# Gated cross-attention with FFN: the way from attention to FFN in halves, and the first query maxima with bv·Wo ahead of the first barrier

## What is computed

```python
# attention, added to x through a gate
q = rope(layernorm(x) @ Wq.T + bq); k = rope(ctx @ Wk.T + bk); v = ctx @ Wv.T + bv
x1 = x + tanh(g_xattn) * ((softmax(q k^T / 4) v) @ Wo.T + bo)
# FFN with fake quantisation, added through a second gate
h  = layernorm(x1)
xq = quant(h, sigmoid(clip_x) * max(abs(h)) / 127)          # ONE maximum over all 8 batches
p  = silu(xq @ quant_rows(w_gate).T) * (xq @ quant_rows(w_up).T)
hq = quant(p, sigmoid(clip_down) * max(abs(p)) / 127)        # again one maximum over everything
out = x1 + tanh(g_ffn) * (hq @ quant_rows(w_down).T)
```

## Time and profile before

| what | value |
|---|---|
| runs shown | 617.42, 615.32, 617.26 us, median 617.26 |
| the profiled execution | 615.77 us, span of its core 614.0 us |
| block A, B, C in the span | 0 to 107.3, 107.6 to 516.1, 516.4 to 614.0 us |
| busy share | PE 90%, DVE 87%, ACT 73%, POOL 43% |
| granted TensorE clock, mean | 0.96 of full |

### The profile page before, as it was taken

One profiled execution on the slowest core, in us unless ns is written; L12 is line 12 of the kernel. 1 busy time (PEld: TensorE's weight loads), 2 busy tenths in 40 slices (PEclk: granted clock), 3 DMA queues, 4 the chain that ended last, 5 costly groups with the idle time before them and its releaser, 6 DMA issues. The chain is left out here.

```text
span 614.0 us, 18320 instructions
## 1 busy us (share of the span) xinstructions
PE 554.1 (90%) x6473; PEld 259.5 (42%) x6478; DVE 531.4 (87%) x679; ACT 445.5 (73%) x886; POOL 263.9 (43%) x372
## 2 busy tenths in 40 slices
PE   6999997899899989999999999999999973988485
PEld 3555654244344424444444444444445321333264
DVE  3899989899999969899899899899899746689888
ACT  2667766247777867897897897897897771788694
POOL 7699996701233434214214314324323210899300
PEclk9999999569999989999999999999999997899889
DMA  8759877523432333242342243253240000000035
GB/s 291 238 164 294 242 203 203 154 55 68 81 65 64 77 61 63 55 89 63 57 89 62 59 86 63 60 85 61 62 90 8 2 2 1 0 2 0 0 104 172
DMA packets 61255, 55.20 MB, mean 90 GB/s; under 512 B 11040, under 2 KB 58784, under 8 KB 61216
## 3 DMA queue, kind: packets, MB, share of 16 engines
q1 hardware_dynamic: 61216, 54.70, 36.1%
HBM read 37.62 MB, written 16.78 MB: 89 GB/s over the span
## 5 line engine op out<-in xcount | busy, mean ns | idle before, releaser
L857 ACT ACTIVATE prob<-st_ps 128x512 f32<-128x512 f32 x512 | 281.2, 596 | 71.9 <-PE st_ps L716 64.9
L916 DVE TENSOR_REDUCE negm<-mx_ps 128x2 f32<-128x1024 f32 x256 | 300.1, 1206 | 17.6 <-PE mx_ps L724 17.4
L716 PE MATMUL st_ps<-q,k 98*32 98x512 bf16 x2048 | 182.5, 385 | 4.4 <-ACT prob L857 4.0
L724 PE MATMUL mx_ps<-k,q 96*32 96x512 bf16 x2048 | 164.8, 396 | 7.5 <-DVE negm L916 3.8
L748 PE MATMUL pv_ps<-prob,v_u 128*32 128x512 f32 x1024 | 133.7, 594 | 1.4 <-ACT prob L857 1.4
L716 PEld LDWEIGHTS st_ps<-q,k 98*32 98x32 bf16 x2048 | 58.6, 96 | 94.6 <-ACT prob L857 40.5
L724 PEld LDWEIGHTS mx_ps<-k,q 96*32 96x32 bf16 x2048 | 55.3, 98 | 79.3 <-DVE negm L916 25.5
L1084 POOL TENSOR_TENSOR msplit<-negm,onesf 128x16 bf16<-128x16 f32 x32 | 7.1, 221 | 135.6 <-DVE negm L916 125.7
L1104 POOL TENSOR_TENSOR normal<-turned,recip 128x256 f32<-128x256 f32 x32 | 19.9, 621 | 79.9 <-DVE recip L930 79.9
L748 PEld LDWEIGHTS pv_ps<-prob,v_u 128*32 128x32 f32 x1024 | 32.1, 111 | 27.3 <-ACT prob L857 3.0
L298 POOL TENSOR_TENSOR parts<-work 128x512 bf16<-128x512 f32 x32 | 38.4, 1206 | 7.1 <-DVE work L286 6.1
(11 more groups left out here) (126 smaller groups left out, 709.5 us busy)
## 6 DMA issues: line engine op xcount, KB each, us to landing
qk_parts<-parts SPq DMA_DIRECT2D x96, 128.0 KB, 2.8
k<-qk_parts SPq DMA_DIRECT2D x192, 64.0 KB, 2.8
q<-qk_parts SPq DMA_DIRECT2D x192, 64.0 KB, 2.9
ctx<-in_ctxT SPq DMA_DIRECT2D x8, 512.0 KB, 4.5
X<-in_x SPq DMA_DIRECT2D x8, 512.0 KB, 7.7
out<-X SPq DMA_DIRECT2D x7, 512.0 KB, 2.9
q<-mrow SPq DMA_DIRECT2D x64, 4.0 KB, 2.5
wf<-in_w_down SPq DMA_DIRECT2D x1, 704.0 KB, 5.0
```

Of the source, the lines that this page charges most:

```text
L716: last = nc.tensor.matmul(score_bank(i)[lo:lo + COLS, :], k6[g][:, h, kt * P + lo:kt * P + lo + COLS], q6[g][:, h, :], start=True, stop=True)
L724: last = nc.tensor.matmul(pair[lo:lo + COLS, qt % 2, :], q6[g][0:ROWS, h, qt * P + lo:qt * P + lo + COLS], k6[g][0:ROWS, h, :], start=True ...
L857: nc.scalar.activation(prob[kt % 2][:, h, :], score_bank(HPU * kt + h)[:], ACT.Exp, scale=SCALE).then_inc(exp_done, 1)
L916: nc.vector.tensor_reduce(negm[g % 2][:, lo:lo + 2], pair[:], op=ALU.max, axis=AX.X, negate=True).then_inc(mx_read, 1)
```

## The change

In block A, after the last projection, GpSimd makes `bv_rep`, TensorE does bv·Wo into a bank of `k_ps` and then the first two pairs of query scores into the banks of `xT_ps` and `v_ps` (which `mx_ps` now is), and ScalarE copies bv·Wo out. In block B VectorE no longer has the two steps of `bo_b`: GpSimd does them, after it has split the maxima of unit 0.

For batch 7, the products with `attnT[0]` are issued in the last unit (`project_last(hf, 0)`), and only those with `attnT[1]` after the last `weigh`. The statistics and normalisation of batch 6 move into the last batch, all on VectorE but `rstd`; ScalarE's eight passes over batch 6, six in the last batch and two behind it, go. Batch 7 is normalised in halves: ScalarE the first two tiles, VectorE the last two, with `rstd` in two halves of two columns on GpSimd.

In block C, chunk 0 is scaled half by VectorE and half by ScalarE, clipped in two halves, transposed into two banks and copied out by ScalarE and VectorE together; chunk 1 is scaled by GpSimd instead of ScalarE.

```diff
@@ block A, TensorE after the last pair of batches
+                pe.wait_ge(bv_ready, KC)
+                pe.wait_ge(rot_ready, 4 * (B - 1) + 2)
+                for c in range(KC):
+                    last = nc.tensor.matmul(k_ps[:, 0, 0:D], bv_rep[:, c, :], wo_raw[:, c, :], start=(c == 0), stop=(c == KC - 1))
+                last.then_inc(wobv_ready, 1)
+                pe.wait_ge(unit_in[0], NLOAD)
+                pe.wait_ge(xnT_ready, KC * B)
+                query_scores(0, 0, 0, mx_ps[0])
+                pe.wait_ge(v_kept, 2 * B)
+                query_scores(0, 0, 1, mx_ps[1])
@@ block A, ScalarE
+                act.wait_ge(wobv_ready, 1)
+                nc.scalar.activation(bo_b[:], k_ps[:, 0, 0:D], ACT.Copy).then_inc(wobv_kept, 1)
@@ block B, TensorE: the last projection in two parts
+                def project_last(hf, c):
+                    dst = project_bank(B, hf)
+                    pe.wait_ge(attnT_ready, 2 * (B - 1) + c + 1)
+                    if c == 0:
+                        pe.wait_ge(x1_ready, 2 * (B - 1))
+                    for t in range(2):
+                        for lo in range(0, P, COLS):
+                            last = nc.tensor.matmul(dst[lo:lo + COLS, t * D:(t + 1) * D], attnT[c][:, (2 * hf + t) * P + lo:(2 * hf + t) * P + lo + COLS], woT[:, c, :],
+                                                    start=(c == 0 and t == 0), stop=(c == KC - 1), skip_group_check=True)
+                    if c == KC - 1:
+                        last.then_inc(wo_ready, 1)
...
+                            if is_last(b) and g == 3 and kt >= 2:
+                                project_last(kt - 2, 0)
...
-                            wait_if(pe, mx_read, 8 * g + 2 * h + j - 1)
-                            query_scores(0, g, h, j, mx_ps[j])
-                        if g == 0 and h >= 2:
...
+                            if g or h:
+                                pe.wait_ge(mx_read, 8 * g + 2 * h + j - 1)
+                                query_scores(g, h, j, mx_ps[j])
...
                 for hf in range(2):
-                    project(B, hf)
+                    project_last(hf, 1)
@@ block B, VectorE
-                dve.wait_ge(wobv_ready, 1)
-                nc.vector.tensor_tensor(bo_b[:], wobv_ps, bo_raw[:], ALU.add).then_inc(bo_ready, 1)
...
-                x1_normalise(B - 2, lambda t: mean[:, TPB * (B - 2) + t:TPB * (B - 2) + t + 1])
-                x1_largest(B - 2)
-                for hf in range(2):
-                    residual(B, hf)
-                    x1_statistics(hf)
...
+                residual(B, 0)
+                x1_statistics(B - 1, (0, 1))
+                residual(B, 1)
+                x1_moments(B - 1, 0)
+                x1_statistics(B - 1, (2,))
+                x1_statistics(B - 1, (3,))
+                dve.wait_ge(tail_scaled, 3)
+                nc.vector.scalar_tensor_tensor(shift1[:], moments1[:, 1, 0:2, 0], -1.0, rstd[:, NT - TPB:NT - TPB + 2], ALU.mult, ALU.mult).then_inc(tail_shift, 1)
+                x1_moments(B - 1, 1)
+                x1_normalise(B - 1, 1)
+                dve.wait_ge(tail_half, 2)
+                x1_half_largest(0)
+                dve.wait_ge(xn_done, TPB * (B - 1) + 2)
+                x1_half_largest(1)
@@ block C, ScalarE, VectorE and GpSimd at its start
-                nc.scalar.activation(xi[1], V[:, 4:8, :], ACT.Copy, scale=ainv[:, 0:1]).then_inc(xs0_ready[1], 1)
-                keep_chunk(0)
+                nc.scalar.activation(xi[0][:, 2:4, :], V[:, 2:4, :], ACT.Copy, scale=ainv[:, 0:1]).then_inc(xs0_ready[1], 1)
+                act.wait_ge(xqT0_ready, 1)
+                nc.scalar.activation(xqT[0][:, 0, :], xqT0_ps[0], ACT.Copy).then_inc(xqT0_kept, 1)
...
-                nc.vector.tensor_scalar(xi[0], V[:, 0:4, :], ainv[:, 0:1], None, ALU.mult).then_inc(xs0_ready[0], 1)
-                clip_x(0, 0)
+                nc.vector.tensor_scalar(xi[0][:, 0:2, :], V[:, 0:2, :], ainv[:, 0:1], None, ALU.mult).then_inc(xs0_ready[0], 1)
                 nc.vector.tensor_scalar(gscale[:], wscale[:, 0:2 * NIC], ascale[:, 0:1], None, ALU.mult).then_inc(gscale_ready, 1)
+                for j in range(2):
+                    dve.wait_ge(xs0_ready[j], 1)
+                    nc.vector.tensor_scalar(xq[0][:, 2 * j:2 * j + 2, :], xi[0][:, 2 * j:2 * j + 2, :], QMAX, -QMAX - 1.0, ALU.min, ALU.max).then_inc(xq0_ready, 1)
+                dve.wait_ge(xqT0_ready, 2)
+                nc.vector.tensor_copy(xqT[0][:, 1, :], xqT0_ps[1]).then_inc(xqT0_kept, 1)
                 clip_x(0, 1)
...
+                pool.wait_ge(ascale_ready, 1)
+                scale_chunk(0, 1)
```

180 lines of the change are left out of this document (110 added, 70 removed).

## The result

The kernel after takes 610.25 us (median of 6 executions, 607.77 to 612.84) against 616.14 (6 executions, 614.09 to 617.42) for the kernel before, run beside it: 0.9909 of the time, 95% interval 0.9886 to 0.9932. That is 5.9 us less where 2.2 were forecast. A second batch with the same kernel gave 610.35, ratio 0.9893 (0.9859 to 0.9928). Two executions of all in this document ran slow and are in no ratio: one of x4_unsplit with 663.01 at a mean granted clock of 0.83, and one of x8_warm_head with 620.59.

The account below looks back on a forecast made before the run. Stretches where one chain runs alone were taken to count, not the steady work. Terms of -2.2, +0.7, -2.3 and +1.6 summed to -2.2: 613.6 us from the profiled 615.77, 614.2 from the mean of 616.4; range 611.4 to 617.3.

Parts of the forecast that it names:

- term 4: Start of the FFN: `gscale` waits on VectorE until GpSimd's scaling of chunk 1 is over, +1.6 us.
- Term 1: Ahead of the first barrier: barrier stays, VectorE's first maximum starts earlier and two gaps go in block B, -2.2 us.
- Rival D: Before the first scores: DMAs of the maxima rows land last, the change is slower, sum +0.3, 616.7 us; chance 0.15.
- Term 2: Last unit: two projection parts in TensorE's order make the last `weigh` start later, +0.7 us.
- Term 3: Tail, from the last projection's start to the last maximum's end: 8.8 instead of 11.13, -2.3 us.
- Rival C: Start of the FFN: GpSimd's scaling does not stop VectorE, -0.9 there, sum -4.7, 611.7 us; chance 0.20.
- Rival B: Tail: TensorE keeps its full clock for the last projection, or the powers are cheap, sum -3.3, 613.1 us; chance 0.20.

Follow-up runs that it names:

- x4_unsplit: Kernel after with the last projection whole behind the last `weigh`, no parts ahead of it: 609.95 us, ratio 0.9882 to the kernel before.
- x8_warm_head: Kernel after with filler matmuls for TensorE at block B's start and between the first maxima: 608.96 us, ratio 0.9873 to the kernel before.
- x2_no_head: Kernel after with `bv_rep`, bv·Wo, bias steps and first two pairs of query scores back in block B: 613.19 us, ratio 0.9946 to the kernel before.
- x10_warm_tail: Kernel after with nine filler matmuls between the last `weigh` and the last projection: 610.87 us, ratio 0.9925 to the kernel before.
- x12: Kernel after with the projection parts needing `attnT[0]` alone behind the last `weigh`, ahead of the others: 608.8 us, ratio 0.9872 to the kernel before.
- x6: Kernel after with twelve extra small VectorE instructions ahead of `gscale` and twelve more in the first pair of chunks: 613.3 us, one execution.
- x9: Kernel after with ScalarE scaling chunk 1 at the FFN's start and no GpSimd instruction there: 609.36 us, ratio 0.9911 to the kernel before.
- x3_no_front: Kernel after with the FFN's start as before (whole chunk 0, chunk 1 scaled by ScalarE): 610.48 us, ratio 0.9901 to the kernel before.
- x7: Kernel after with batch 0's means made ahead of GpSimd's rounding of the FFN weights in batch 1: 606.87 us, ratio 0.9834 to the kernel before.
- x14_early_means: Repeat of x7, kernel after with batch 0's means ahead of GpSimd's rounding of the FFN weights: 605.58 us, ratio 0.9823 to the kernel before.

## Why the prediction was wrong

The measured 610.25 lies below the range of 611.4 to 617.3. The sum was -2.2. By the table's columns, with the low clock at 221 of the same length in both kernels, it should have been -2.0 + 0.7 - 2.7 - 0.1 = -4.1. The step that failed is term 4, which alone makes 1.7 of the difference to the measured -5.9; it would have led to 612.5. Another 0.2 is the net of the other terms, and 1.8 stands in no term.

- **Term 1, head, -2.2: right as far as it went.** 22.74 became 20.50 to 20.94, so -1.8 to -2.2. The 16 maxima run without a gap, and the barrier moved by 0.3, the tenths by which the last query projection ended later. Rival D did not come. The sum took `bv_rep` at its old 0.76; it took 1.65, hidden.
- **Term 2, last unit, +0.7: right.** With the low clock alike (before 374.06, x2_no_head 374.74, x10_warm_tail 374.81) it is +0.7, and the last units alone show 20.64 for 20.02. What I did not ask was whether it had to be paid: x12 does the same work behind the `weigh`, where the tail is no longer for it (11.41 against 11.37 at the full clock), and the last units take 19.29.
- **Term 3, tail, -2.3: -2.7 in the first profile, -2.5 in the second.** The residuals came 1.46 and 3.17 behind the projection's start (I had 1.75 and 3.5 to 4.2), and the power of two columns took 0.69 (I had 0.6). Where the clock stayed at full it was -3.4, the end that the prediction had for it.
- **Term 4, start of the FFN, +1.6: the step that failed.** It came out at -0.1. The prediction said that `gscale` stands still until GpSimd's scaling is over. It was held for 0.9 only and was let in 1.4 behind that instruction's start, 1.7 before its end. I had carried over what the rows show beside a product of GpSimd to another kind of instruction, and taken the page's rule as support. The Trainium skill (SBUF — State Buffer, "Who interferes with whom") has the loser wait for the whole instruction. The trace contradicts it for this pair: 1.09 for `gscale` and two clips at 0.28 each beside the rest. x6 shows the form of it: VectorE is kept out at the start and again at the end of GpSimd's instruction, and let in between, where the whole of this chain's work happened to fit. That it fitted is luck of these lengths. Rival C had the right direction, but its -0.9 supposes no hold at all, and came only in x9, with GpSimd's instruction gone. As that hold of 0.9 eats what the half chunks gain, term 4 came to nothing.
- **What no term held: TensorE's granted clock.** From 4.1 to the measured 5.9 there are 1.8, and the intervals of the ratios (4.2 to 7.0 us less, and 4.4 to 8.7 in the second batch) leave it open how many of them are real. The profiles show three places. At 221 all three profiles without the head's part, but with the wait, have the low clock, for 3.4 each; of the nine profiles with both (x8_warm_head among them) five have none and four have it for 3.4 or 6.8. Three against nine is few, and on average over these nine it comes to some 0.4 less. Behind the barrier, before has 0.6 more in the first piece in one of its two profiles. In the FFN, from the first weights to the end, before's two profiles take 92.64 and 93.31 and after's two 92.89 and 92.31, 0.4 less on average. The mean granted clock of an execution cannot count the falls at 221, as it adds up all low stretches: x10_warm_tail has 0.966 with a fall there, x3_no_front 0.963 without. x7 shows that the fall needs the wait. Why it should be rarer when block B starts 2 us earlier is not shown, nor that it is; I know no step of the kernel that tells it. So about 1 of the 1.8 can be named and the rest stays open.

Rival B's mechanism is real too: in x2_no_head, x6_probe_scale, x8_warm_head and x14_early_means the clock stayed at its full level through the last projection, and the third column is 0.7 to 1.1 shorter. With the wait left empty it comes by luck of the execution. x12's order may make it likelier, with three profiles of three against four of eleven, which is too few to be sure.

## What to carry to other kernels

Look for the longest wait in the whole trace, also where the change does nothing: here a 4 us instruction of GpSimd stood ahead of two 0.2 us ones that ScalarE and then TensorE waited for, and moving it was worth more than any one part of the change. Before splitting work to put it ahead of a critical instruction, see whether the same work fits into the wait behind it. And price an operation by a row of its own kind: a standstill seen beside one kind of instruction says nothing of another. When a probe is repeated, look at the single ones in their order; a median of twelve hid that five of them stood still.

## What the runs showed of the hardware

- GpSimd's `tensor_scalar` of 128x1024 f32 to int16 (2.86 to 3.15) kept VectorE's small SBUF instructions out for 1.1 to 1.4 from its start, let them in for some 0.8, and kept them out again over its last 0.9 to 1.0 (x6_probe_scale, twice), whereas a clip that met products waited to their end.
- TensorE's granted clock fell from 1.00 to 0.50 behind a wait of 3.2 in seven profiles of twelve, and in none of the five in which that wait was gone. A fall cost 1.2 to 1.4 us when it lasted 3.4, and 2.4 to 2.6 when it lasted 6.8. Between the same two instructions of attention (unit 8 to unit 30, 251.75 to 252.01) where no fall lies, seventeen profiles agree within 0.3.
- At a barrier the clock also fell with filler running (x8_warm_head, the one profiled execution of six), and TensorE's filler then cost 10 us.
- GpSimd's power took 0.69 for two columns and 1.01 for four: a line through the two has about half of the 0.69 independent of the columns, by an estimate. Beside VectorE's work it took up to 0.89.
- GpSimd's `bv_rep`, a product of 128x128, took 0.40 each at the start of block B and 0.84 each beside VectorE's two-input instructions in block A.
